# Layer 0's attention: output, query and key products moved to other row tiles' slots of the head, with their additions and copies

## The reference

```python
xqkv = x @ Wqkv
xq = rope(xqkv[..., :q_size].reshape(B, S, H, D))
xk = rope(xqkv[..., q_size:q_size + kv_size].reshape(B, S, KV, D))
xv = xqkv[..., q_size + kv_size:].reshape(B, S, KV, D)
scores = jnp.einsum('bhsd,bhtd->bhst', q, k) * D ** (-0.5)
probs = jax.nn.softmax(scores + mask[None, None], axis=-1)
att = jnp.einsum('bhst,bhtd->bshd', probs, v).reshape(B, S, H * D)
return att @ Wo            # x = x + ga * this
```

## Time and profile before

| | us |
|---|---|
| median of 3 runs | 795.38 (795.17 to 795.42) |
| profiled execution | 796.95 |
| its span, first to last instruction | 795.1 |
| PE busy in the span | 724.7 (91%) |
| DVE, ACT, POOL busy | 569.1, 451.9, 387.0 |

### The profile page before, as it was taken

The page is one execution under the profiler, slowest core; times in us unless marked ns, Lnnn a source line. Parts: engine busy times, 40 slices in busy tenths (PEclk is TensorE's granted clock), DMA queues, the critical chain, the costliest instruction groups (busy, mean ns, idle before and its releaser), DMA issues. The chain is left out here.

```text
span 795.1 us, 12529 instructions
## 1 busy us (share of the span) xinstructions
PE 724.7 (91%) x4436; PEld 626.6 (79%) x4436; DVE 569.1 (72%) x1281; ACT 451.9 (57%) x923; POOL 387.0 (49%) x412
## 2 busy tenths in 40 slices
PE   5797999999999999999999778996989999889997
PEld 4576888888888888888888668996777778667787
DVE  4456767677776787667877798987578887666667
ACT  3355666666666676666665424431668876646432
POOL 5692685535855367553450260041525554304873
PEclk9988999999999999999999998998999999999999
DMA  6000000000000000004000220001300000000001
GB/s 244 1 14 8 14 9 20 14 8 14 21 15 7 7 14 14 14 10 165 7 14 1 84 49 1 2 1 35 125 1 0 2 0 1 1 4 0 2 2 54
DMA packets 19084, 19.87 MB, mean 25 GB/s; under 512 B 2126, under 2 KB 16974, under 8 KB 19022
## 3 DMA queue, kind: packets, MB, share of 16 engines
q1 hardware_dynamic: 18206, 18.41, 7.2%
q10 hardware_dynamic: 816, 0.66, 0.2%
HBM read 18.01 MB, written 1.05 MB: 24 GB/s over the span
## 5 line engine op out<-in xcount | busy, mean ns | idle before, releaser
L880 POOL TENSOR_TENSOR at_swapped<-at_swapped,at_sin 128x512 f32<-128x512 f32 x40 | 51.6, 1291 | 136.6 <-ACT at_swapped L603 136.6
L625 ACT ACTIVATE at_probs<-at_probs,at_negmax 128x128 f32<-128x128 f32 (+7 forms) x128 | 99.6, 778 | 28.6 <-DVE at_negmax L709 26.7
L709 DVE CUSTOM_DVE_ANT_0 at_probs<-at_scores,causal 128x128 f32<-128x128 f32 (+7 forms) x128 | 96.1, 751 | 16.8 <-PE at_scores L59 16.2
L518 PE MATMUL at_turn<-ident_sb,at_probs 128*128 128x128 f32 x576 | 85.8, 276 | 15.2 <-DVE at_full_T_lo L725 14.2
L518 PEld LDWEIGHTS at_turn<-ident_sb,at_probs 128*128 128x128 f32 x576 | 67.0, 141 | 24.1 <-issue 11.9
L618 ACT ACTIVATE at_edge_T_hi<-at_turn 128x128 fp32r<-128x128 f32 (+3 forms) x128 | 55.6, 434 | 35.4 <-PE at_turn L518 35.0
L57 PE MATMUL at_scores<-at_kT_hi,room 128*128 128x512 f32 (+1 forms) x192 | 66.8, 348 | 4.4 <-DVE at_v L691 3.5
L58 PE MATMUL at_scores<-at_kT_lo,room 128*128 128x512 f32 (+1 forms) x192 | 66.9, 348 | 0.0
L618 ACT ACTIVATE at_full_T_hi<-at_turn 128x512 fp32r<-128x512 f32 x64 | 38.2, 597 | 50.1 <-PE at_turn L518 48.1
L59 PE MATMUL at_scores<-at_kT_hi,room 128*128 128x512 f32 (+1 forms) x192 | 66.4, 346 | 0.0
L725 DVE TENSOR_TENSOR at_edge_T_lo<-at_turn,at_edge_T_hi 128x128 fp32r<-128x128 f32 (+3 forms) x128 | 61.4, 480 | 1.4 <-ACT at_edge_T_hi L618 1.0
(11 more groups left out here) (405 smaller groups left out, 2377.6 us busy)
## 6 DMA issues: line engine op xcount, KB each, us to landing
at_wq_in<-L_attn_Wqkv SPq DMA_DIRECT2D x16, 128.0 KB, 2.2
at_wo_in<-L_attn_Wo SPq DMA_DIRECT2D x16, 128.0 KB, 2.0
staging<-L_ffn_routed_w SPq DMA_DIRECT2D x7, 256.0 KB, 4.9
ff_wmod<-L_wmod SPq DMA_DIRECT2D x1, 1536.0 KB, 6.4
at_wmod<-L_wmod SPq DMA_DIRECT2D x1, 1024.0 KB, 7.7
staging<-L_ffn_w_gate SPq DMA_DIRECT2D x1, 1024.0 KB, 5.1
staging<-L_ffn_w_up SPq DMA_DIRECT2D x1, 1024.0 KB, 7.1
staging<-L_ffn_w_down SPq DMA_DIRECT2D x1, 1024.0 KB, 9.5
```

What stands on the lines that cost most here:

```text
L518: mm = pe.transpose(p_turn[t % 2][:, b - b0, :], probs[:, s % 4, b * P:(b + 1) * P], m.ident[:, :])
L625: act.activation(row, row, ACT.Exp, scale=-1.0, bias=negmax[:, unit % 4:unit % 4 + 1], accum_out=rowsum[:, unit // NT % 2, i:i + 1])\
L709: dve.tensor_tensor_reduce(out=probs[:, s % 4, 0:width], in0=p_scores[s % 2][:, 0:width], in1=m.causal[:, S - width:], scale=-1.0, scalar= ...
L880: pool.tensor_tensor(swapped[:, r % 2, :], swapped[:, r % 2, :], sin[:, cols], ALU.mult).then_inc(rope_turned, 1)
```

## The change

The places of the products in the head are now two tables and a list. Output products go to slots 2, 3, 5 and 6 (before 4 to 7), query halves to slots 1 and 2 (before 0 and 1), the key's halves to slot 3 (before 1). In a slot the key product now stands ahead of `attend`; query and output products stand behind it as before. The special place ahead of the scores in heads 4, 8 and 12 is gone. ACT's copies and DVE's multiplications and additions go with their products, POOL's rotations too. On POOL `split_o` now stands ahead of the slot's rotation.

The rest of the diff replaces several semaphores of POOL by one chain that counts on (`m.pool_chain`); an instruction that waited for the one before it on POOL still does, and none is added or taken away (the ffn parts have the same edit).

```diff
-        QUERY_UNITS, KEY_SLOTS, KEY_SPLIT = (0, 1), [(1, 1), (2, 1)], (0, 5)
+        QUERY_SLOTS, OUT_SLOTS, KEY_SLOTS, KEY_SPLIT = {1: 0, 2: 1}, {2: 0, 3: 1, 5: 2, 6: 3}, [(1, 3), (2, 3)], (0, 5)
...
         def out_here(g, h, i):
-            return i >= 4 and (g, h) != (0, 0)
+            return i in OUT_SLOTS and (g, h) != (0, 0)
...
                 def slot(g, h, i):
                     head = g * PER_KV + h
                     unit = head * NT + i
-                    if i == 0 and h == 0 and g:
-
-                        pe.wait_ge(exp_done, unit - 1)
-                        query_job(head + 1, 0, query_bank(0))
                     scores(g, h, i)
                     if unit < 4:
                         value_job(4 + unit)
                     if unit >= 2:
                         turn(unit - 2)
+                    if key_here(g, h, i):
+                        pe.wait_ge(proj_free, use_number["key", g + 1, h - 1])
+                        key_job(g + 1, h - 1, p_proj[:, :])
                     if i in (2, 3) and head:
                         attend(head - 1, 1, 4 * (i - 2), 4 * (i - 1))
                     if i == 6:
                         attend(head, 0, 0, 4)
-                    if query_here(g, h, i) and not (i == 0 and h == 0 and g):
+                    if query_here(g, h, i):
+                        c = QUERY_SLOTS[i]
                         if head == 0:
-                            pe.wait_ge(v_lo, 2 * i + 2)
-                        query_job(head + 1, i, query_bank(i))
-                    if key_here(g, h, i):
-                        pe.wait_ge(proj_free, use_number["key", g + 1, h - 1])
-                        key_job(g + 1, h - 1, p_proj[:, :])
+                            pe.wait_ge(v_lo, 2 * c + 2)
+                        query_job(head + 1, c, query_bank(c))
                     if out_here(g, h, i):
-                        pe.wait_ge(proj_free, use_number["out", head - 1, i - 4])
-                        out_job(head - 1, i - 4)
+                        pe.wait_ge(proj_free, use_number["out", head - 1, OUT_SLOTS[i]])
+                        out_job(head - 1, OUT_SLOTS[i])
...
                 def slot(g, h, i):
                     head = g * PER_KV + h
+                    if i == 0 and head:
+                        split_o(head - 1)
                     if query_here(g, h, i):
-                        query_turn(head + 1, i)
+                        query_turn(head + 1, QUERY_SLOTS[i])
                     if key_here(g, h, i):
                         key_turn(g + 1, h - 1)
-                    if i == 0 and head:
-                        split_o(head - 1)
...
```

More of the change, by code:

```diff
@@ L138, in build @@
         m = Shared(x, ident, causal, modcol, gate, stats, meanvar, vareps, rstd, tiny, hT,
-                   staging, staging1, staged, staged1, gate_w, expert_bias, gate_in, mod_row, tables, w2_gated, room, sqrt_in, sqrt_out, chain, nbias, csil, ones, staging_at)
+                   staging, staging1, staged, staged1, gate_w, expert_bias, gate_in, mod_row, tables, w2_gated, room, sqrt_in, sqrt_out, chain, nbias, csil, ones, staging_at, pool_chain)
         attention0(nc, a, m, sems, sb, split)
@@ L342, in query_here @@
         def query_here(g, h, i):
-            return i in QUERY_UNITS and (g, h) != last_head
+            return i in QUERY_SLOTS and (g, h) != last_head
         def key_here(g, h, i):
@@ L355, in attention0 @@
             if query_here(g, h, i):
-                ropes.append(("query", g * PER_KV + h + 1, i))
+                ropes.append(("query", g * PER_KV + h + 1, QUERY_SLOTS[i]))
             if key_here(g, h, i):
@@ L360, in attention0 @@
             if out_here(g, h, i):
-                uses.append(("out", g * PER_KV + h - 1, i - 4))
+                uses.append(("out", g * PER_KV + h - 1, OUT_SLOTS[i]))
         rope_number = {r: n for n, r in enumerate(ropes)}
@@ L636, in slot @@
                     unit = head * NT + i
-                    if i == 0 and h == 0 and g:
-                        copy_rope(rope_number["query", head + 1, i], query_bank(i))
                     if unit >= 2:
@@ L643, in slot @@
                         value_hi(4 + unit)
+                    if key_here(g, h, i):
+                        copy_rope(rope_number["key", g + 1, h - 1], p_proj[:, :])
                     if i == 3 and head:
@@ L647, in slot @@
                         attended_hi(head, 0)
[L648 to L651, removed]
+                    if query_here(g, h, i):
+                        copy_rope(rope_number["query", head + 1, QUERY_SLOTS[i]], query_bank(QUERY_SLOTS[i]))
                 def scale_shift(n):
@@ L764, in slot @@
                         value_lo(4 + unit)
+                    if key_here(g, h, i):
+                        cos_rope(rope_number["key", g + 1, h - 1], h - 1, p_proj[:, :], proj_free)
                     if i == 3 and head:
@@ L768, in slot @@
                         attended_lo(head, 0)
[L769 to L772, removed]
+                    if query_here(g, h, i):
+                        c = QUERY_SLOTS[i]
+                        cos_rope(rope_number["query", head + 1, c], c, query_bank(c), query_free)
                     if out_here(g, h, i):
-                        add_out(head - 1, i - 4)
+                        add_out(head - 1, OUT_SLOTS[i])
                     if unit == 5:
@@ L843, in _ @@
             def _(pool):
-                weights = Chain(pool, w_hi)
+                chain = m.pool_chain.on(pool)
                 def split_weights(staged, out, ready):
-                    weights.run(pool.tensor_scalar(out.hi, staged, 1.0, 1.0, ALU.mult, ALU.mult))
+                    chain.run(pool.tensor_scalar(out.hi, staged, 1.0, 1.0, ALU.mult, ALU.mult))
                     pool.tensor_tensor(out.lo, staged, as_f32(out.hi), ALU.subtract).then_inc(ready, 1)
@@ L868, in split_o @@
                         pool.wait_ge(gates_done, 1)
-                    pool.tensor_tensor(wo_in[:, :], wo_in[:, :], m.gate[:, 0, 0, :], ALU.mult).then_inc(wo_gated, 1)
+                    chain.step(pool.tensor_tensor(wo_in[:, :], wo_in[:, :], m.gate[:, 0, 0, :], ALU.mult))
                     if head:
                         pool.wait_ge(out_mm, head * 4)
-                    pool.wait_ge(wo_gated, head + 1)
+                    chain.settle()
                     split_weights(wo_in[:, :], wo, wo_ready)
@@ L936, in _ @@
                 pool.wait_ge(scores_mm, KV0 * UNITS - NT)
-                pool.tensor_scalar(w.hi, w_in, 1.0, 1.0, ALU.mult, ALU.mult).then_inc(ffn_w_hi, 1)
+                chain.step(pool.tensor_scalar(w.hi, w_in, 1.0, 1.0, ALU.mult, ALU.mult))
                 split_o(H0 - 1)
                 pool.wait_ge(scores_mm, KV0 * UNITS)
-                pool.wait_ge(ffn_w_hi, 1)
+                chain.settle()
                 pool.tensor_tensor(w.lo, w_in, as_f32(w.hi), ALU.subtract)
@@ L1238, in _ @@
                     rows = wd_in[:, c * DM:(c + 1) * DM]
-                    pool.tensor_tensor(rows, rows, m.gate[:, 0, 1, :], ALU.mult).then_inc(wd_gated, 1)
-                pool.wait_ge(wd_gated, I0 // P)
+                    chain.step(pool.tensor_tensor(rows, rows, m.gate[:, 0, 1, :], ALU.mult))
+                chain.settle()
                 flat = wd("p c d -> p (c d)")
-                pool.tensor_scalar(flat.hi, wd_in, 1.0, 1.0, ALU.mult, ALU.mult).then_inc(wd_hi, 1)
-                pool.wait_ge(wd_hi, 1)
+                chain.run(pool.tensor_scalar(flat.hi, wd_in, 1.0, 1.0, ALU.mult, ALU.mult))
                 pool.tensor_tensor(flat.lo, wd_in, as_f32(flat.hi), ALU.subtract).then_inc(wd_ready, 1)
@@ L1249, in _ @@
                         .then_inc(hx_ready, 1)
-                chain = Chain(pool, signed)
                 pool.wait_ge(mod_read, 3)
@@ L1708, in _ @@
             def _(pool):
-                chain = Chain(pool, sem("wo_chain"))
+                chain = m.pool_chain.on(pool)
                 pool.wait_ge(m.staged1, 80)
```

36 lines of the change are left out of this document (17 added, 19 removed).

## The result

The changed kernel takes 831.7 us (median of 4 runs, 829.83 to 833.22) against 795.4 us: a ratio of 1.0455, 95% interval 1.043 to 1.048. Forecast were 828 us, in a range of 813 to 838.

The account below looks back on a forecast made before the run. The prediction took PE, busy 91% of the span and idling mostly for DVE's low parts, as the bound; its terms over the heads summed to 33.0 us on the median 795.38, giving 828 us, range 813 to 838.

Parts of the forecast that it names:

- The border: Between heads: tile 6's and 7's turns at M (tile 7's maximum begins) +1.98 and +4.11; net loss 1.86 us.
- Heads without a key half: Slots 0 to 7 of these heads: 1.8 us more each in 3, 7, 11, 13, 14; 1.2 in 4, 8, 12.
- M came late: Slots 4 to 7 without a key half: DVE starts tile 7's maximum some 0.5 us after PE, bounds 0 and 1.
- Heads 4, 8, 12: Start of these heads: tile 7's turn loses its 1.48 us wait and comes 1.53 earlier, yet 0.75 is lost.
- Key heads: Slots 2 and 3: key waits 1.4 us for an addition, next output product 0.3; with the border 3.5 per head.
- rival (b): Borders of heads: new waits halve the clock at each of 14, 3.4 us a fall, 876 us; chance 0.08.
- Head 1, head 0 and the ends: Outside the regular heads: head 1 costs 2.4 us, head 0 nothing, the end of the loop gains 0.3.
- (a): Only the border costs time; neither the key nor slot 6 waits: 814 us; chance 0.12.
- (c): Border turns begin earlier and PE's waits of 0.37, 1.48 and 2.8 us vanish: 785 us; chance 0.03.
- (d): Full slots: PE's work there has hidden slack and it evens out, 795 us; chance 0.03.
- (e): POOL late with the query, or DVE behind in slots 2 and 3: 1 us more per head, 842; chance 0.04.
- No cost on POOL: POOL, all heads: same instructions, busy half the time, earlier `split_o`, merged semaphores guarding the same waits; no cost.

Follow-up runs that it names:

- e6_filled: Changed kernel plus seven matmuls of empty work per head, from head 1 on, in slots 0 and 1: 826.0 us.
- e1: Changed kernel with the output products back in slots 4 to 7; queries and key stay moved: 809.5 us.
- e2: Changed kernel with the query halves back in slots 0 and 1, without the special place in heads 4, 8, 12: 810.54 us.
- e9: e5_plain with the four output products one slot earlier, in slots 3 to 6: 809.01 us.
- e7: PE as in e5_plain; copies, cosines and rotations of queries in slots 1 and 2, of the key in slot 3: 796.58 us.
- e8: As e7 in heads without a key half, as e5_plain in head 0 and the key heads: 791.0 us.
- e5_plain: Kernel before with only the special place in heads 4, 8 and 12 taken away: 793.27 us.
- e3: Changed kernel with only the key halves back in slot 1, behind the first query half: 826.0 us.
- e4: Changed kernel with slot 2's output product ahead of the query half and its addition ahead of the cosines: 830.92 us.

## Why the prediction was right, step by step

The steps and their waits came out as forecast; how near the sum came, 828 for 831.7, is partly luck. Without the falls of the clock, heads 2 to 15 would have cost 27.4 us by their periods, where the sum had 30.9; the falls, which the sum left out, added 5.2. The two errors have opposite signs.

- **The border.** Tile 6's and tile 7's turns at M + 1.98 and M + 4.11 were forecast, M + 1.97 and M + 4.10 measured, within 0.02 in heads 2 to 15; the reading of head 15 as the case without filling carried the whole sum. e6_filled shows that the time is free on PE, e1 and e2 that the two fillings count separately (0.47 and 0.62, 1.08 together, up to slot 7's scores), e9 that one of them does so alone.
- **Heads without a key half:** forecast 1.8 (3, 7, 11, 13, 14) and 1.2 (4, 8, 12) more per head, measured 1.43 and 0.84. The mis-sized terms are small ones. M came late by 0.35, not 0.5: tile 6's turn waits 1.43 in these heads and 1.08 in those behind a key head. The old wait in slot 2 was worth 0.57, not 0.5, as e7 and e8 show. The terms add up to 1.86, and 1.8 is that rounded down; nothing was added for the wait of 0.1 that the line of the sum speaks of. The remaining 0.2 is what the moved products cost less where they went: between their starts and the next product's, an output product takes 0.72 behind a query half and 0.83 behind a turn.
- **Heads 4, 8, 12:** that the wait of 1.48 goes and doesn't pay was right; e5_plain has what it is worth alone, 0.59 per head.
- **Key heads:** forecast 3.5, measured 3.42. The wait for the addition was forecast at 1.4 and recorded as 1.16, the second at 0.3 and recorded as 0.15; from start to start, against the kernel before, they are 1.41 and 0.23. e3 takes only 1.44 of these 1.64 back, since M comes late by 0.35 once they are gone; with them it did not. The step's cause, "that addition is queued behind the second query half's multiplication", is right for the larger part: e2, which has no query half there, leaves 0.31 and 0.22. So some 1.1 of the 1.64 is that queue, and 0.5 is one bank for two products within a slot of each other. e4 doesn't take the queue away, it changes which product meets it.
- **The clock** was rival (b), at 0.08, with the remark that one or two falls lie in the range. There were four, for 5.2 us (1.55, 1.58 and 1.31 in heads 5, 7 and 14, and 0.75 in head 15, which has 24.17 here and 23.42 in e6). The rival's price of 3.4 us for one fall was too high: it came from a stretch of 6.8 us, and each of these lasts 3.4. The clock is the one term left out of the sum, and more than makes up for the 3.5 us by which the heads were forecast too long. PE's busy time, forecast unchanged, is also higher in the traces with falls (731.8 to 733.9) than in those of e1 and e2 (727.0 and 729.9). My argument from head 15, three short waits with no fall, took the absence of falls in few cases for their absence: the fall comes in only some borders of the same kind. The rule of the Trainium skill cited there ("TensorE: Matmul & The Clock Gate", "A second HAM failure mode: psum-queue depth-cycling") agrees with e6 in kind, short repeated idles do make the clock fall; the 876 us that the prediction worked out for it was not measured, as the clock fell at 4 of 14 borders.
- **Head 1, head 0 and the ends:** heads 0 and 1 cost 0.5 and 2.8 (forecast 0 and 2.4), of which the 0.5 is within the spread of head 0 between traces; in e6 head 1 is 1.1 shorter than here. The stretch after head 15's M got 0.5 shorter (forecast 0.3). By the profiled executions: 0.5 + 2.8 + 32.55 (heads 2 to 15) - 0.5 = 35.3, the difference of the spans 830.4 and 795.1. Forecast were 33.0.
- **Rivals.** (a), 814, is out: the key's wait is there. (c) and (d) are out with the two turns. Of (c), the wait of 1.48 did go, but e5_plain prices it at 0.59 per head. Its count of 9 waits of 0.37 is too low, the trace of before has 11; the 785 would be 784. Of (e) nothing showed: no wait of PE names POOL, and no head without a fall of the clock lost more than forecast.
- **No cost on POOL** was right: e8 has the changed kernel's merged semaphores and its earlier `split_o`, and its key heads take 24.80 to 24.83, as in e5_plain, which has the old ones.
- **A reading:** "nearly all of its idle time in this attention, 14.2 us in 18 waits" holds from 79 to 400 us, where 8.1 of the 9.1 us that PE is idle are such waits; in the whole loop, from 41 to 437 us, other recorded waits add up to 6.6 beside the 14.2. Nothing in the sum hangs on it.

## What to carry to other kernels

In a software pipeline in which small and large steps follow one another, look for the step at which the other engines' chain is longest and the matrix engine's own share smallest: independent products placed there are free, and the wait recorded there (0.37 us) is only what the filling leaves over. Find its full size where the filling happens to be missing (here the last head) before moving anything. Two products that share a bank want their reader between them: in e4, taking away the wait of one handed it to the next user of the bank, and e1, e7 and e9 each met a wait at this bank, of 0.3 to 0.5 us, that their forecasts had not counted. And where a reader's copy stands may be set per case: deferring it gained 0.57 us in heads without a key product and lost 0.67 in those with one.

## What the runs showed of the hardware

- The clock fell to 1.2 GHz for 3.4 us behind pairs of waits of 1.1 to 1.4 and 0.8 us (2.60 of 4 us busy before one of them), but only at 4 of 14 such borders, and at 4 of 14 again in e3 and e4; it did not fall in heads 2 to 15 of e1, e2 and e9, which have one of the two waits at full length (both only in head 15 of e2 and e9). One fall cost 0.8 to 1.6 us. With 7 empty matmuls in each pair it did not fall once there, and the kernel was 5.7 us faster with 7 x 15 matmuls more.
- Waits of PE at a bank of up to some 0.35 us were missing in its matmul rows (e7, e9) and longer ones were recorded 0.16 to 0.25 too short (e1, the changed kernel). They show in full as a longer distance from one start to the next, and the rows of the weight loads name them (0.35 to 0.39).
